# Row transform of the last row pairs in two parts, stacked inverse rows and a reordered convolution in a two-layer image kernel

## The reference, cut to what is computed

```python
# layer 0: masked 3x3 convolution to 32 hidden channels, ReLU, 1x1 back to 8
x = x + conv_preact(group_norm(x))
# layer 1: Fourier operator, 4 groups, width 10, on group_norm(x) and two grid channels
h = gconv1x1(concat(group_norm(x), grid), fc0)
for i in range(4):
    xf = rfft2(h)[24 row modes, 12 column modes]
    h1 = irfft2(einsum('bgixy,gioxy->bgoxy', xf, spectral_w[i]))
    h = h1 + gconv1x1(h, w[i])
    if i < 3: h = h * sigmoid(h * sp) / 1.1          # a scaled silu
h = gswish(gconv1x1(h, fc1)); x = x + gconv1x1(h, fc2) # 10 -> 128 -> 2 per group
```

## Time and profile before

| what | value |
|---|---|
| median of three runs | 18805.97 us |
| lowest, highest | 18733.34, 18934.47 us |
| the profiled execution: its own time | 18689.34 us |
| its span, first to last instruction | 18687.5 us |
| mean granted TensorE clock (1 is 2.4 GHz) | 0.931 |
| busy: PE, PEld, DVE, ACT, POOL | 91%, 37%, 32%, 60%, 0% |

### The profile page before, as it was taken

One profiled execution on the slowest core, in us unless ns is written; L12 is line 12 of the kernel. 1 busy time (PEld: TensorE's weight loads), 2 busy tenths in 40 slices (PEclk: granted clock), 3 DMA queues, 4 the chain that ended last, 5 costly groups with the idle time before them and its releaser, 6 DMA issues.

```text
span 18687.5 us, 558642 instructions
## 1 busy us (share of the span) xinstructions
PE 17071.6 (91%) x246998; PEld 6964.5 (37%) x246998; DVE 5971.9 (32%) x7496; ACT 11286.9 (60%) x10628; POOL 55.3 (0%) x69
## 2 busy tenths in 40 slices
PE   4999999999999999999999999999999999999999
PEld 2334433344433344333443334433344433344333
DVE  4223332233322333223333223332233322333222
ACT  1665556655566655666556665556665566655666
POOL 0000000000000000000000000000000000000000
PEclk8999989998999999999999999999999999989999
DMA  1111111111111111111111111111111111111111
GB/s 39 37 30 38 33 34 40 33 35 31 37 36 37 31 36 32 36 39 29 37 33 36 37 33 36 32 34 39 37 31 33 34 36 39 29 36 32 37 37 30
DMA packets 507240, 648.66 MB, mean 35 GB/s; under 512 B 90082, under 2 KB 482362, under 8 KB 488646
## 3 DMA queue, kind: packets, MB, share of 16 engines
q1 hardware_dynamic: 502246, 610.43, 12.6%
q10 hardware_dynamic: 2408, 0.28, 0.0%
HBM read 476.10 MB, written 134.29 MB: 33 GB/s over the span
## 4 chain that ended last, share of the span: by engine, by line
PE 87%; DVE 5%; issue 3%; DVEq 3%; ACT 1%; ACTq 1%; SPq 0%; DMA 0%
PE PS L695 23%; PE PS L710 22%; PE PS L665 10%; PE PS L657 9%; PE PS L593 7%; PE PS L490 4%; PE PS L541 3%; PE PS L571 3%; PE PS L614 2%; DVEq L1053 2%; PE PS L566 2%; PE PS L499 1%; DVE work L1041 1%; DVE work L805 1%; PE PS L515 1%
## 5 line engine op out<-in xcount | busy, mean ns | idle before, releaser
L793 ACT ACTIVATE work<-PS 128x512 f32<-128x512 f32 (+1 forms) x8192 | 7937.9, 1021 | 714.3 <-PE PS L695 203.3
L695 PE MATMUL PS<-hmem,f1w 31*128 31x512 f32 x32768 | 4685.5, 641 | 104.6 <-DVE hmem L1099 42.9
L710 PE MATMUL PS<-work,f2w 128*32 128x512 f32 x32768 | 4378.9, 606 | 37.9 <-ACT work L793 36.2
L786 ACT ACTIVATE hmem<-PS 128x2048 f32<-128x2048 f32 x1056 | 1983.0, 1878 | 1783.6 <-PE PS L665 1783.6
L1041 DVE STREAM_TRANSPOSE work<-hmem 128x2048 f32<-128x2048 f32 x1056 | 2440.9, 2311 | 1425.9 <-ACT hmem L786 712.8
L695 PEld LDWEIGHTS PS<-hmem,f1w 31*128 31x128 f32 x32768 | 1282.8, 183 | 3484.2 <-ACT work L793 3366.1
L665 PEld LDWEIGHTS PS<-invc,gst 24*128 24x128 f32 x22528 | 1545.8, 330 | 1380.3 <-issue 1362.3
L665 PE MATMUL PS<-invc,gst 24*128 24x256 f32 x22528 | 2057.1, 482 | 0.0
L763 ACT ACTIVATE gst<-PS 128x528 f32<-128x528 f32 (+1 forms) x384 | 206.9, 539 | 2860.6 <-PE PS L566 1619.5
L710 PEld LDWEIGHTS PS<-work,f2w 128*32 128x32 f32 x32768 | 650.5, 108 | 3184.2 <-ACT work L793 3045.6
L1105 DVE SCALAR_TENSOR_TENSOR work<-PS,f2b,work 128x512 f32<-128x512 f32 x224 | 168.2, 751 | 4597.8 <-PE PS L710 4597.8
(11 more groups left out here) (124 smaller groups left out, 7651.0 us busy)
## 6 DMA issues: line engine op xcount, KB each, us to landing
work<-in_x SPq DMA_DIRECT2D x1518, 128.0 KB, 2.5
wspec<-in_spec_w SPq DMA_DIRECT2D x768, 90.0 KB, 2.1
hmem<-x_d SPq DMA_DIRECT2D x128, 528.0 KB
x_d<-work SPq DMA_DIRECT2D x512, 128.0 KB, 2.9
wspec<-in_spec_w SPq DMA_DIRECT2D x768, 60.0 KB, 2.0
work<-x_d SPq DMA_DIRECT2D x384, 64.0 KB
wspec<-x_d SPq DMA_DIRECT2D x384, 64.0 KB
out_x<-work SPq DMA_DIRECT2D x384, 64.0 KB
```

What stands on the lines that cost most here:

```text
L695: mm = nc.tensor.matmul(PS[:, fc_bank(p, r), :], f1w[32 * r:32 * r + 31, k, g, :], hmem[32 * r:32 * r + 31, g * PART + u * ROW2:g * PART + ...
L710: mm = nc.tensor.matmul(PS[32 * c:32 * c + 32, 7, :], f2w[:, k, g, :], act[p % 2][:, c * ROW2:c * ROW2 + ROW2], start=kg == 0, stop=final, ...
L786: nc.scalar.activation(unit(u), PS[:, at:at + 4, :], ACT.Silu).then_inc(s_hrow, 1)
L793: nc.scalar.activation(act[p % 2][:, strips], PS[:, bank:bank + (3 if rest else 1), :].rearrange("p a b -> p (a b)"), ACT.Silu).then_inc(s ...
```

## The change

- **Convolution.** PE's order becomes two shifts of `conv1(u)`, then `conv2(u-1)`, then the third shift. ReLU of the second pair of banks moves to VectorE (`relu`), in front of its transposes. The wait for the image before moves to unit 1.
- **Sums.** `summed` writes four strips of the two t: the modes, and below them the swapped and negated modes, by three matmuls per t and s (one of 120 columns, two of 60). `mixed` loses the swapping instructions.
- **Inverse rows.** Cosine and sine are stacked: 40 matmuls of 56 rows on strips of 64, where there were 80 of 24 rows.
- **Forward transform.** Units 8 and 9 are transformed in one part (`columns_b`, 64 matmuls) and unit 10 in another (`columns_c`, 32), each on four column tiles; each part is turned and row-transformed (`rows_b`, `rows_c`, 12 matmuls each). The row transform of units 0 to 7 moves behind the column parts. The silu and the turn of unit 10 are done in two halves.
- **Unit 9's own place.** It is the memory of `f1w` and `f2w`, now one tile `fcw`, which is saved to DRAM once and loaded again in each image.

```diff
+        fcw = sb("fcw", [128, 2048])
+        singles = [... for part in (work[:, 16384:18432], fcw[:, 0:2048], work[:, 2048:4096])]
...
                 sp_.wait_ge(s_ot, i * 4 + 4)
+                sp_.dma_start(fcw[:, 0:FCW], fcw_d[:, :]).then_inc(s_fcw, 16)
                 residual(0)
...
-                conv1(0)
                 for u in range(UNITS):
-                    if u + 1 < UNITS:
-                        conv1(u + 1)
-                    conv2(u)
+                    pe.wait_ge(s_z, i * UNITS + u + 1)
+                    pe.wait_ge(s_x1, i * UNITS + u + (HEAD_X1 - 1))
+                    if u == 1:
+                        pe.wait_ge(s_fo, i * PU + HEAD_FO)
+                    pe.sem_inc(s_bank, 1)
+                    conv1(u, 1)
+                    conv1(u, 0)
+                    if u:
+                        conv2(u - 1)
+                    conv1(u, 2).then_inc(s_mm1, 1)
+                conv2(UNITS - 1)
...
+                def summed(bank, g, pick, terms, first, last):
+                    to = PS[:, bank, 120 * g:120 * g + 120].rearrange("p (o r k) -> p r o k", o=5, r=2)
                     for s in range(2):
-                        mm = nc.tensor.matmul(to, weights, by[:, :, t:WID:4, :, s], ..., tile_position=(0, 32 * t))
+                        for t in range(2):
+                            nc.tensor.matmul(to[64 * t:64 * t + 32], sums[:, 0, pick, :], by[:, :, t:WID:2, :, s], ...
+                                             tile_position=(0, 64 * t))
+                            for r in range(2):
+                                mm = nc.tensor.matmul(to[64 * t + 32:64 * t + 64, 1 - r], sums[:, r, pick, :],
+                                                      by[:, r, t:WID:2, :, s], ..., tile_position=(0, 64 * t + 32))
...
                         for g in range(G):
-                            for cs in range(2):
-                                for a in range(count):
+                            for a in range(count):
+                                p, ch = 64 * (a % 2), 5 * g + 2 * t + a // 2
+                                ... rot[p:p + 32 + KX, ch, ...], invr[p:p + 32 + KX, ...], start=True, stop=True
...
+                def columns_b(lay):
+                    pe.wait_ge(s_tr, i * TR + lay * PU + UNITS + 2)
+                    pe.wait_ge(s_ft, i * FT + 3 * lay + 2)
+                    for b in range(4): for j in range(4): for r in range(4):
+                        mm = column(singles[j // 2], 4 * (j % 2) + b, j, r, 4, 0, 2, b == 0, b == 3)
+                def columns_c(lay):
+                    pe.wait_ge(s_tr, i * TR + lay * PU + PU)
+                    for b in range(2): for j in range(4): for r in range(4):
+                        mm = column(singles[2], 2 * j + b, j, r, 0, 256, 2, b == 0, b == 1)
+                def transform(lay):
+                    columns_b(lay)
+                    columns_c(lay)
+                    pe.wait_ge(s_ft, i * FT + 3 * lay + 3)
+                    rows(lay, rows_a, 2, 0)
+                    rows(lay, rows_b, 1, 2)
+                    pe.wait_ge(s_ft, i * FT + 3 * lay + 4)
+                    rows(lay, rows_c, 1, 3).then_inc(s_f, 1)
...
+                        if lay < LAYERS - 1 and u == PU - 1:
+                            nc.scalar.activation(unit(u)[:, 0:2], PS[:, at:at + 2, :], ACT.Silu).then_inc(s_half, 1)
+                            nc.scalar.activation(unit(u)[:, 2:4], PS[:, at + 2:at + 4, :], ACT.Silu).then_inc(s_hrow, 1)
...
+            def relu(i, u):
+                bank = 4 * (u % 2) + 2
+                dve.wait_ge(s_mm1, i * UNITS + u + 1)
+                V.tensor_scalar(hid[u % 2][:, 1024:2048], PS[:, bank:bank + 2, :]..., c1b[:, 0:1], 0.0, ALU.add, ALU.max)
...
                 V.drain().then_inc(s_x1, 1)
+                if u + 1 < UNITS:
+                    relu(i, u + 1)
                 V.transpose(acts[:, cols], xt[:, cols]).then_inc(s_t0, 1)
...
-                    for u in range(UNITS + 1):
+                    for u in range(UNITS + 2):
                         turn(i, lay, u)
-                    turn(i, lay, 9)
-                    turned_rows(lay, False)
-                    turn(i, lay, 10)
-                    turned_rows(lay, True)
+                    turned_rows(lay, rows_a, 4, 0, 4)
+                    turn_last(i, lay)
+                    turned_rows(lay, rows_b, 4, 0, 2)
+                    turned_rows(lay, rows_c, 0, 256, 2)
```

More of the change, by code:

```diff
@@ L23 @@
 CHUNKS = 8
+FCW1 = 3 * G * FF
+FCW = FCW1 + 3 * G * 32
 NBLK = 3
@@ new lines, in inverse_rows, with column, columns_a @@
+                        mm.then_inc(s_g, 1)
+                def column(part, b, j, r, bank, at, yy, first, last):
+                    to = PS[32 * j:32 * j + 24, bank + r, at:at + 128 * yy].rearrange("p (s k y) -> p s y k", s=4, y=yy)
+                    return nc.tensor.matmul(to, fcol[32 * r:32 * r + 32, b, :], part[32 * r:32 * r + 32, :, :, b, :], start=first,
+                                            stop=last, tile_position=(32 * r, 32 * j))
+                def columns_a(lay):
+                    pe.wait_ge(s_tr, i * TR + lay * PU + UNITS)
+                    pe.wait_ge(s_hrow, i * (4 * PU) + (lay * PU + 9))
@@ L586, in columns @@
                     pe.sem_inc(s_bank, 1)
-                    many, yy = (3, 2) if last else (4, 4)
                     for b in range(8):
-                        for j in range(many):
+                        for j in range(4):
                             for r in range(4):
-                                part = singles[j] if last else pairs[j]
-                                to = PS[32 * j:32 * j + 24, 4 + r, 0:128 * yy].rearrange("p (s k y) -> p s y k", s=4, y=yy)
-                                mm = nc.tensor.matmul(to, fcol[32 * r:32 * r + 32, b, :],
-                                                      part[32 * r:32 * r + 32, :, :, b, :], start=b == 0, stop=b == 7,
-                                                      tile_position=(32 * r, 32 * j))
+                                mm = column(pairs[j], b, j, r, 4, 0, 4, b == 0, b == 7)
@@ new lines, in columns_c, with rows @@
+                def columns_c(lay):
+                    pe.wait_ge(s_tr, i * TR + lay * PU + PU)
+                    pe.sem_inc(s_bank, 1)
+                    for b in range(2):
+                        for j in range(4):
+                            for r in range(4):
+                                mm = column(singles[2], 2 * j + b, j, r, 0, 256, 2, b == 0, b == 1)
+                    mm.then_inc(s_col, 1)
+                def rows(lay, part, halves, step):
+                    turned = part.rearrange("p (c h f) -> p c h f", c=CH, h=halves)
+                    for h in range(halves):
@@ L625, in mode_sums @@
                             strips = [a for a in range(4) if group_of(a, n) == g]
-                            weights = sums[:, 4 if len(strips) == 4 else 5 + strips[0] // 2, :]
+                            pick = 4 if len(strips) == 4 else 5 + strips[0] // 2
                             first = n == 0 or group_of(0, n - 1) < g and group_of(3, n - 1) < g
                             last = n == WID - 1 or group_of(0, n + 1) > g
-                            for t in range(4):
-                                mm = summed(weights, 1, t, g, ring[n % 4], first, last)
+                            mm = summed(1, g, pick, ring[n % 4], first, last)
                         mm.then_inc(s_sum, 1)
@@ L670, in pixels @@
                         if u == 9 and lay < LAYERS - 1:
-                            columns(lay, False)
+                            columns_a(lay)
                     if lay < LAYERS - 1:
-                        rows(lay, False)
-                        columns(lay, True)
-                        rows(lay, True)
+                        transform(lay)
                 spin(2, 3)
                 pe.wait_ge(s_pr, i * PR + 1)
-                for t in range(4):
-                    for g in range(G):
-                        mm = summed(sums[:, g, :], 6, t, g, acc, True, True)
+                for g in range(G):
+                    mm = summed(6, g, g, acc, True, True)
                 mm.then_inc(s_sum, 1)
```

206 lines of the change are left out of this document (101 added, 105 removed).

## The result

The changed kernel takes 17727.57 us (median of four runs, 17673.44 to 17773.97); the kernel before, run beside it, 18769.65. The ratio, taken from fast runs alone, is 0.9482 with a 95% interval of 0.9458 to 0.9505; the two medians as they stand give 0.9445. That is 5.2% less by the ratio, where 4.2% was forecast. Either way it is near the rival "better clock" (17,810 or less), not near the likeliest case (18,010). The profiled executions differ by 18689.34 - 17673.44 = 1016 us, 31.7 us an image.

What follows compares the result with a forecast made beforehand. TensorE's chain was 87% of the span, the dense silu on ScalarE untouched. Terms of -28.8 us an image, less 4.1 for lower clock, left 24.7 x 32 = 790 us: 17,899, times 1.0062 gives 18,010 us; range 17,790 to 18,480.

Steps and rivals of the forecast that it cites:

- Convolution: Convolution stage: idle wait for the residual goes, period 3.82 us a unit, columns begin 5.3 us earlier an image.
- Forward transform: Transform behind three layers: shorter PE stops, row matmuls end at +9.2 us after unit 10's silu begins; -15.6 us an image.
- better clock: Rival: no stretch falls to the lower clock, nor do layer 0's units; gain 31 us an image, 17,810 or less; 8%.
- likeliest case: Whole kernel: 18,010 us, own range 17,810 to 18,260, a fifth of rows and sums at the lower clock; 61%.
- this rival: Rival in the convolution: tiling-mode drains keep up to 0.95 us of each gap; 19.4 us an image gained, 18,180; 4%.
- Strips side by side: Sums: four strips run together, 0.40 us a call; the rival had them not, 1.6 us a call, 19,460; 3%.
- inverse rows: Inverse rows of four layers: stacked matmuls save 5.5 us an image, range 2 to 7.
- units *stuck* at the lower level: Rival: pixel units stay at the lower clock, +8 us each in layers 0 and 2; 18,525; 8%.
- allowance of 4.1 us: Transform rows and layer sums: a fifth of them at the lower clock, 4.1 us an image taken off the gain.
- layer sums, hidden: 0: Layer sums: twelve calls take 4.8 us at the upper clock, hidden under VectorE's products of 5.77 us; change 0.
- sign that the prediction named for the lower clock: Layer sums: they end about 0.6 us after the last product; later would mean the lower clock.
- first modes: First columns to first inverse rows: 1.5 us less an image, with the first column transform at its old time.

Runs made afterwards that it cites:

- x9_whole: Changed kernel with the last unit's silu and turn of layers 0 to 2 in one piece each; 17802.65 us.
- x1_unstacked: Changed kernel with inverse rows again as two accumulated 24-row matmuls on four row strips, sine side left out; 18284.15 us.
- x3_sums8: Changed kernel with two 60-column matmuls of the sums joined into one of 120, swap and sign left out, 8 matmuls a call; 17513.00 us, ratio to before 0.9364.
- x5_turned: Changed kernel with 8 matmuls a call in the sums, one writing in turned order, signs applied by the VectorE operation; 17479.19 us, ratio to before 0.9294.
- x11_before_spin: Kernel before the change with four spin matmuls in place of three in front of even layers' inverse rows; 18557.62 us, ratio to before 0.9866.
- x7_spin2: Changed kernel with two spin matmuls in place of three in front of even layers' inverse rows; 17949.88 us.

## Why the prediction was right, and where not

**Forward transform: right, in size and in its steps** (-16.1 for -15.6). Each time reckoned from the silu of unit 10 was within 0.25 us. `x9_whole` prices the halves at 0.7 us of a layer's 5.4 and shows the wait that they remove.

**Convolution: right, size a little off** (-4.7 for -5.3). The columns were forecast 36.7 us behind the first `conv1`, and begin at 36.69. The gain is smaller because image 17, from which it was reckoned, took 41.99 us before, where the mean is 41.36. Inside the stage two misses cancel, which is luck: the period is 3.92 instead of 3.82 (six of them, +0.6), and the first `conv2` begins 6.69 us behind the first `conv1` instead of 7.24 (-0.55). `conv1` with `conv2` in its middle takes 2.99 us where it took 2.83. The Trainium skill, TensorEngine Tiling (Array Packing), "Tiling Modes", says that a change of mode drains the engine; whatever of that is in the period is at most 0.10 us a unit, against the 0.95 that this rival allowed. What the prediction did not say is that the two edits are worth nothing singly.

**Reload: right**, hidden. **Strips side by side: right.** Twelve matmuls, 960 columns, take 0.44 us a call, near the 0.40 forecast and far from the 1.6 of the rival. The Trainium skill, TensorE: Matmul & The Clock Gate, "The mechanism" in Part 3, says that a weight load overlaps running matmuls only where the row groups differ. All four strips share their rows, and twelve matmuls with their loads still took 0.44 us, so these rows do not agree with it.

**The failed step: the clock behind the inverse rows.** The prediction left the units at their old time (0 for layers 0 and 2), put a rival with the units *stuck* at the lower level at 8% and gave "better clock" 8%, with some 2 us an image for layer 0's units in its gain of 31. It had read 0.50 throughout in one of two images and spoke of "some images"; the record of the clock shows it in the units of layer 0 in all 30 images before, 16.8 us an image, and in those of layer 2, 8.2 us. Its reason was that fewer records precede the units, so that the level might fall more. `x1_unstacked` shows the opposite: without the stacked matmuls the level is lost in every image, and holding it is worth 5.5 us in the units of layer 0 and 3.4 in those of layer 2, and 1.9 and 2.4 in their inverse rows. The same error made the inverse rows too small (-7.9 for -5.5): the prediction priced layer 0's at the lower level, and they run at the upper one. The allowance of 4.1 us for a fifth of the rows and sums at the lower level was not needed: the transforms ran at the upper level in every image. Together the better clock was worth about 9.7 + 2.4 + 4.1 = 16 us against the likeliest case.

**The second failed step: "layer sums, hidden: 0".** The speed of a call was right (0.44 us), the sum was not, since it counted columns and never instructions. It is +4.5 in the stage against -0.9, and +1.7 in the units behind it. `x3_sums8` and `x5_turned` show that this goes with the number of matmuls at the same columns. The sign that the prediction named for the lower clock, sums that end over 0.6 us after the last product, showed at the upper level: it was the instructions. So the forecast came within 1 to 1.6% in part by luck, by two errors that partly cancel, 16 us too pessimistic on the clock and 7 us too optimistic on the sums.

**A smaller miss: the first modes** (-0.7 for -1.5). The first column transform was left at its old time. It took 175.6 us of PE's time where it took 146.2, 0.9 us an image more (mean 496 ns for 410), and the stage holds 8.6 us of the lower level an image for 4.8 before. Why the level is lower there was not looked into.

**Not looked into:** the dense stage, 1.1 us an image longer. The record of the clock has 4.2 us of the lower level there for 1.5 before; no run takes that apart.

## What to carry to other kernels

Count instructions as well as columns: when several short matmuls run side by side on column strips, price a call by its entries too, and look for stops with no releaser. Read the granted clock of the stage *behind* an edit: merging matmuls into fewer that use more rows, and shortening the standstill in front of them, can bring more in the stage that follows than in the one that was edited. Where an edit moves work between engines and another reorders it, undo each alone before crediting either.

## What the runs showed of the hardware

- TensorE stopped about 1.0 us, 96 times, in sums of 48 entries (matmuls and weight loads) a call of 0.44 us, and once with 32 entries a call (`x5_turned`). Each of the 96 stops ended 1.24 to 1.51 us after a 16 KB packet of the instruction queue had landed.
- With a standstill of only 0.36 us in front, the 80 inverse-row matmuls of 24 rows were followed by the lower clock in the units of layer 0 in every image (`x11_before_spin`). With the 40 of 56 rows this happened in 0 to 15 of 30 images after 0.73 to 0.75 us, depending on the kernel around them, and in 15 of 30 after 1.58 us (`x7_spin2`).
- A matmul that writes its output in turned order took as long as the plain one beside it (283 ns mean each in `x5_turned`), and a product out of PSUM takes VectorE as long as a copy (658 and 657 ns for 480 columns).
